# A macaron transformer block (feed-forward, attention, feed-forward) on one core: the list of dense steps by engine clocks in nanoseconds, and six bursts of value products a group for seven

## The chip, the cores and the metric

One core of a Trainium2 chip runs one program. The metric is the device time of an execution in microseconds, the median of the runs shown. The kernel stays in one launch.

## The reference

```python
x = x + 0.5 * ffn(layernorm(x))
x = x + attention(layernorm(x))
x = x + 0.5 * ffn(layernorm(x))            # x: 16 x 1024 x 256, float32

def ffn(x):                                # x_prev: x one position earlier, zeros at the start
    xr = mu_r * x + (1 - mu_r) * x_prev
    xk = mu_k * x + (1 - mu_k) * x_prev
    return sigmoid(xr @ W_r.T) * (square(relu(xk @ W_k.T)) @ W_v.T)

def attention(x):                          # 16 heads of 16, rotary embedding on q and k, causal
    q, k, v = split(x @ W_qkv + b_qkv)
    att = softmax(mask(rope(q) @ rope(k).T / 4))
    return (att @ v) @ W_proj + b_proj
```

## The kernel before

**Attention sets the beat.** Time is laid out in slots, numbered from `FIRST` = -120. A batch has 16 heads in 4 groups of 4; a group has 12 ticks (a block of 128 keys against a block of 512 queries, cut at the diagonal), and each tick 4 slots, one for each head. So a group is 48 slots and a batch 192, 3072 in all. In a slot TensorE makes one score block (`score`, L704, 512, 384, 256 or 128 columns of bf16, with the negated row maximum as extra rows), and one block of the maxima pass of a coming group (`maximum`, L714, the same widths, 13 slots ahead). Scores go to one of NS = 2 PSUM banks (`ps_s`), and ScalarE takes their exponential to `pt_sb` (L830). Maxima go to one of NM = 3 banks (`ps_m`); VectorE takes the row maximum (L943 at the diagonal, L946 elsewhere). GpSimd zeroes what lies above the diagonal (L1075).

**Value products** (`pv`, L735) run in bursts given by `BURSTS`: a burst makes the products of one or two ticks for 4 heads, three slots after the last of its ticks. They are float32, of 32-column weights, and four heads stand side by side in the array. `PT` = 3 tick buffers hold the exponentials.

**Dense steps** fill the rest. All that is not attention's own beat is a step with a name: statistics (`f_st0`, `a_st0`), the reciprocal root on GpSimd (`f_rstd`), normalising on ScalarE to `xt_sb` (`f_x0`, `f_x1`), a transpose (`f_T`, `a_T`, L742), mixing with the position before (`f_dif`, `f_k0` to `f_r1`), the feed-forward matmuls `f_K` (L788), `f_R` (L791) and `f_V` (L794), query and key `r_QK` (L800), value `a_V` (L804), projection `p_P` (L781), the rotary steps (`r_swap`: four DMAs that swap halves, L612; `r_cos`, `r_sin` L997, `r_add` L1001), the split of q and k in three bf16 parts, and DMAs that spread them to rows (`rows`, L627, two each). Each matmul step on a chunk of 256 positions is four units, a unit being 128 x 128 weights on 256 columns, float32, that the profile shows as two matmuls. They use one of ND = 2 PSUM banks, and an ACT or DVE step empties each.

**The planner.** `Plan.describe` (L126) gives every step an engine, a cost in slots, an earliest slot (its release less 16) and the steps it follows, each with a lag in slots. `Plan.place` goes through the slots; every engine earns credit (`RATE`, of TensorE 1.0 a slot) and spends it on the first step by rank whose lags have passed. The outcome is one fixed order for each engine. Each engine's program walks the slots: TensorE does the slot's score, its maximum, the dense units placed there, then a burst if one is due; ScalarE the exponential and then dense steps; VectorE dense steps and then the maximum; GpSimd the diagonal and then dense steps; SP only dense steps, which are DMAs. The planner's times are no waits: at run time each engine waits on semaphores, in order.

## Time and profile before

| | us |
|---|---|
| median of the runs | 3116.66 |
| lowest of the runs | 3114.29 |
| profiled execution, device time | 3112.07 |
| its span, first to last instruction | 3110.3 |

The granted TensorE clock of the profiled execution is 0.991 on the mean. One microsecond is 0.03% of the span. The profile's rows give start, length, engine, line and what is written from what; TensorE's matmuls overlap, since each one is pipelined behind the next, so the distance between starts tells what one costs.

### The profile page before, as it was taken

How to read it: one execution, taken by the hardware profiler on the slowest of the kernel's cores; microseconds unless marked ns; L12 is line 12 of the kernel's file. 1: busy time of each engine (PE TensorE's matmuls, PEld its weight loads, DVE VectorE, ACT ScalarE, POOL GpSimd, SP SyncE). 2: the span in 40 equal slices, each digit the busy share in tenths (PEclk: the TensorE clock that was granted, in tenths of full speed). 3: DMA queues.
4: the chain of work that ended last, by engine and by line, in shares of the span. 5: the costliest groups of instructions: out<-in, count | busy, mean ns of one | idle time of the engine just before them, and what ended most of it. 6: DMA issues, size and time to landing. Idle time of an engine off the chain costs nothing.

```text
span 3110.3 us, 56224 instructions
## 1 busy us (share of the span) xinstructions
PE 2962.3 (95%) x18245; PEld 1665.9 (54%) x18245; DVE 2475.0 (80%) x7302; ACT 2159.2 (69%) x4802; POOL 1566.6 (50%) x2190
## 2 busy tenths in 40 slices
PE   6899999999999999999999999999999999999997
PEld 4444555555555555555555555555555555555444
DVE  3888888888888888888888887888888888887872
ACT  4477777777777777777777777777767777777664
POOL 5455555555455455555555455454555555454323
PEclk9899999999999999999999999999999999999999
DMA  3443343343434352342443333343442532433421
GB/s 99 79 84 65 64 100 66 83 90 72 86 77 88 69 97 67 76 99 60 91 87 68 88 77 84 80 85 76 79 93 59 98 81 67 93 76 71 83 60 39
DMA packets 202585, 245.49 MB, mean 79 GB/s; under 512 B 68405, under 2 KB 104245, under 8 KB 202293
## 3 DMA queue, kind: packets, MB, share of 16 engines
q1 hardware_dynamic: 202293, 241.90, 37.5%
q8 instruction: 146, 2.39, 0.4%
q14 instruction: 146, 1.20, 0.2%
HBM read 53.48 MB, written 51.38 MB: 34 GB/s over the span
## 4 chain that ended last, share of the span: by engine, by line
PE 66%; DVE 12%; ACT 8%; POOL 6%; issue 6%; DMA 1%; SPq 1%; POOLq 0%; DVEq 0%; ACTq 0%
PE ps_y L735 14%; PE ps_s L704 12%; PE ps_m L714 11%; PE ps_d L794 7%; PE ps_d L788 6%; PE ps_d L791 5%; PE ps_d L800 5%; ACT pt_sb L830 4%; DVE ps_m L943 3%; PE ps_d L781 3%; PE ps_d L742 2%; DVE mx_sb L946 2%; PE ps_d L804 2%; POOL pt_sb L1075 2%; DVE dif_sb L974 2%
## 5 line engine op out<-in xcount | busy, mean ns | idle before, releaser
L830 ACT ACTIVATE pt_sb<-ps_s 128x512 f32<-128x512 f32 (+1 forms) x3039 | 1451.6, 495 | 816.9 <-PE ps_s L704 806.7
L943 DVE CUSTOM_DVE_ANT_0 ps_m<-ps_m,mask_sb 128x128 f32<-128x128 f32 (+3 forms) x2048 | 990.3, 498 | 370.7 <-PE ps_m L714 355.9
L704 PE MATMUL ps_s<-qr_sb,kr_sb 99*128 99x512 bf16 (+1 forms) x3039 | 994.5, 329 | 50.4 <-ACT pt_sb L830 39.3
L714 PE MATMUL ps_m<-kr_sb,qr_sb 96*128 96x512 bf16 (+3 forms) x3072 | 1000.1, 329 | 37.9 <-DVE mx_sb L943 27.7
L946 DVE TENSOR_REDUCE mx_sb<-ps_m 128x1 f32<-128x512 f32 x1024 | 697.9, 682 | 105.7 <-PE ps_m L714 97.3
L1075 POOL TENSOR_SCALAR_AFFINE_SELECT pt_sb<-pt_sb 128x512 f32<-128x512 f32 x512 | 331.4, 647 | 833.8 <-ACT pt_sb L830 833.3
L735 PE MATMUL ps_y<-pt_sb,v_sb 128*32 128x512 f32 (+3 forms) x6144 | 589.9, 494 | 3.6 <-POOL pt_sb L1075 2.7
L704 PEld LDWEIGHTS ps_s<-qr_sb,kr_sb 99*128 99x128 bf16 x3039 | 291.8, 96 | 510.0 <-issue 229.7
L714 PEld LDWEIGHTS ps_m<-kr_sb,qr_sb 96*128 96x128 bf16 x3072 | 302.0, 98 | 319.2 <-DVE mx_sb L943 71.1
L800 PE MATMUL ps_d<-axn_sb,wqk_sb 128*128 128x256 f32 x1024 | 305.3, 396 | 3.9 <-ACT axn_sb L872 3.9
L735 PEld LDWEIGHTS ps_y<-pt_sb,v_sb 128*32 128x32 f32 x6144 | 154.6, 109 | 285.9 <-issue 258.3
L788 PE MATMUL ps_d<-ka_sb,wk_sb 128*128 128x256 f32 x1024 | 305.1, 395 | 0.5 <-DVE ka_sb L968 0.5
L791 PE MATMUL ps_d<-wr_sb,dif_sb 128*128 128x256 f32 x1024 | 303.1, 383 | 0.1
L794 PE MATMUL ps_d<-wv_sb,ka_sb 128*128 128x256 f32 x1024 | 301.3, 383 | 0.3 <-ACT dif_sb L865 0.3
L943 DVE DVE_READ_ACCUMULATOR2_ANT mx_sb<- 128x1 f32 x2048 | 286.7, 140 | 0.0
L1116 POOL TENSOR_TENSOR qb_sb<-qb_sb,cos_sb 128x512 f32<-128x512 f32 x124 | 176.2, 1421 | 129.7 <-DMA sw_sb<-qb_sb 129.6
L788 PEld LDWEIGHTS ps_d<-ka_sb,wk_sb 128*128 128x128 f32 x1024 | 189.8, 197 | 52.7 <-issue 2.3
L1103 POOL TENSOR_TENSOR x_sb<-x_sb,dif_sb 128x512 f32<-128x512 f32 x128 | 162.7, 1271 | 100.5 <-DVE dif_sb L980 100.0
L794 PEld LDWEIGHTS ps_d<-wv_sb,ka_sb 128*128 128x128 f32 x1024 | 179.6, 190 | 44.4 <-ACT fxn_sb L854 4.9
L1122 POOL TENSOR_TENSOR part_sb<-qb_sb,part_sb 128x512 bf16<-128x512 f32 x124 | 145.2, 1171 | 114.8 <-ACT part_sb L894 114.3
L800 PEld LDWEIGHTS ps_d<-axn_sb,wqk_sb 128*128 128x128 f32 x1024 | 177.0, 193 | 46.8 <-issue 4.3
L791 PEld LDWEIGHTS ps_d<-wr_sb,dif_sb 128*128 128x128 f32 x1024 | 177.3, 191 | 44.8 <-DVE dif_sb L980 0.5
(96 smaller groups left out, 3465.5 us busy)
## 6 DMA issues: line engine op xcount, KB each, us to landing
kr_sb<-part_sb SPq DMA_DIRECT2D x378, 128.0 KB, 4.4
qr_sb<-part_sb SPq DMA_DIRECT2D x378, 128.0 KB, 4.7
y_way<-yt_sb SPq DMA_DIRECT2D x128, 256.0 KB, 2.7
sw_sb<-qb_sb SPq DMA_DIRECT2D x496, 64.0 KB, 2.0
x_sb<-x SPq DMA_DIRECT2D x64, 256.0 KB, 2.8
yn_sb<-y_way SPq DMA_DIRECT2D x64, 256.0 KB
den_sb<-r_way SPq DMA_DIRECT2D x64, 256.0 KB
out<-x_sb SPq DMA_DIRECT2D x64, 256.0 KB, 2.2
```

What stands on the lines that cost most here:

```text
L704: eng.matmul(score_bank(slot)[:, 0:width], kr_sb[0:KR + NP, n % RS, j, kb * P:(kb + 1) * P], qr_sb[0:KR + NP, n % RS, j, q0:q0 + width], s ...
L714: eng.matmul(ps_m[:, u % NM, 0:width], qr_sb[0:KR, n % RS, j, i * P:(i + 1) * P], kr_sb[0:KR, n % RS, j, piece * QC:piece * QC + width], s ...
L735: pv_j = eng.matmul(ps_y[32 * j:32 * j + 32, QC - width:QC], v_sb[:, b % 2, kb, col:col + 32], pt_sb[:, buffer, j, column:column + width], ...
L788: mm = eng.matmul(ps[:, rows], wk_sb[:, cc, cols], ka_sb[:, i % 2, cc, :], start=(cc == 0), stop=(cc == CC - 1))
L791: mm = eng.matmul(ps[:, rows], dif_sb[:, i % 2, cc, cols], wr_sb[:, cc, :], start=(cc == 0), stop=(cc == CC - 1))
L794: mm = eng.matmul(ps[:, rows], ka_sb[:, i % 2, cc, cols], wv_sb[:, cc, :], start=(cc == 0), stop=(cc == CC - 1))
L800: mm = eng.matmul(ps[:, rows], wqk_sb[:, cc, w0:w0 + P], axn_sb[:, c, cc, :], start=(cc == 0), stop=(cc == CC - 1))
L830: eng.activation(pt_sb[:, buffer, j, column:column + width], score_bank(slot)[:, 0:width], ACT.Exp, scale=SCALE).then_inc(exped, 1)
L943: eng.tensor_tensor_reduce(ps_m[:, u % NM, 0:width], ps_m[:, u % NM, 0:width], mask_sb[:, m0:m0 + width], 1.0, -3e38, ALU.add, ALU.max, be ...
L946: eng.tensor_reduce(best, ps_m[:, u % NM, 0:width], mybir.AxisListType.X, ALU.max).then_inc(max_taken, 1)
L1075: eng.affine_select(out=diag, in_=diag, compare_op=ALU.is_ge, fill=0.0, base=0, pattern=[[0, G], [1, P]], channel_multiplier=-1).then_inc( ...
L1116: eng.tensor_tensor(biased_of(i), biased_of(i), cos, ALU.mult).then_inc(r_cos, 1)
```

## The change

`BURSTS` loses one entry: ticks 0 and 1 of a group go out together.

`Plan.place` is written anew from slot `SWITCH` = 48 on. Up to there the old placing is kept (`place_early`, with the old tests renamed `can_make_at` and `ready_at`). Behind it each engine has a clock in nanoseconds. `TAKES` gives for every step the time that the engine is held and the time after which others see it done; `EXP` and `MAX` give the same for the exponentials and the row maxima, and TensorE's own work goes by columns at 2.36 GHz, with 245 ns a burst. In a slot the new `place` advances TensorE past the score and the maximum (each no sooner than its bank is free by the clocks), places a transpose if its input is seen and a bank is free (`turn`), and then units (`unit`): one if there is one, and more for as long as the next score's or maximum's bank comes free over 150 ns later. The other engines are filled (`fill`) with steps whose predecessors are seen by then, up to a limit and with a slack (`SLACK`): a lower step goes to VectorE only if it ends within 400 ns of the next maximum's being made. `f_R` may now follow the start of `f_K`, `f_V` that of `f_R`, and `y_copy` follows its burst. Some releases move earlier by 4 to 14 slots. The checks that rows and maxima are placed some slots ahead are gone; in their place the clock waits for them. `READER` is renamed `EMPTIER`.

```diff
--- before.py
+++ after.py
@@ -47,7 +47,7 @@
 BSLOTS = NG * GSLOTS
 PV_AT = 3
 PT = 3
-BURSTS = [(0,), (1,), (2, 3), (4, 5), (6, 7), (8, 9), (10, 11)]
+BURSTS = [(0, 1), (2, 3), (4, 5), (6, 7), (8, 9), (10, 11)]
 PLACES = [(k, 0) if TICKS[k][1] != KQ * TICKS[k][0] + KQ - 1 else (k - 1, QC // 2) for k in range(NTK)]
 OWNERS = [k for k in range(NTK) if PLACES[k][0] == k]
@@ -58,6 +58,7 @@
 NH = KQ * G
 UNITS_FIRST = [(i, j, piece) for i in (3, 0, 2, 1, 7, 4, 6, 5) for j in range(G) for piece in range(i // KQ + 1)]
 FIRST = -120
+SWITCH = 48
 HALF_MAX = -53
 REST_MAX = -33
@@ -83,8 +84,24 @@
 class Plan:
 
+    TAKES = {"f_st0": (335, 470), "f_st1": (600, 760), "f_rstd": (1600, 1700), "f_x0": (490, 645), "f_x1": (490, 645), "f_T": (440, 640),
+             "f_xn": (477, 645), "f_dif": (1270, 1330), "f_k0": (397, 530), "f_k1": (397, 530), "f_r0": (397, 530), "f_r1": (397, 530),
+             "f_relu": (477, 665), "f_sq": (500, 675), "f_tanh": (477, 645), "f_u": (600, 735), "f_xadd": (1222, 1330),
+             "a_st0": (335, 470), "a_st1": (600, 760), "a_rstd": (1600, 1700), "a_x0": (490, 645), "a_x1": (490, 645), "a_T": (440, 640),
+             "a_xn": (477, 645), "a_vc": (477, 645), "a_bias": (1222, 1330), "r_b0": (356, 530), "r_b1": (356, 530), "r_swap": (240, 3600),
+             "r_cos": (1350, 1700), "r_sin": (700, 840), "r_add": (603, 740), "r_hi": (519, 680), "r_rest": (1170, 1500), "r_mid": (519, 680),
+             "r_low": (1170, 1500), "store": (60, 2500), "load": (60, 3800), "h_fin": (700, 900), "h_T": (130, 400), "h_copy": (156, 330),
+             "h_rows": (240, 2500), "m_fin": (900, 1000), "m_T": (130, 400), "m_copy": (157, 330), "m_rows": (60, 2500),
+             "y_copy": (477, 645), "y_out": (120, 3500), "y_recip": (159, 300), "y_back": (60, 2700), "y_in": (120, 4500),
+             "y_mul": (1300, 1400), "xp": (604, 740), "b_add": (328, 450)}
+    EXP = {128: (157, 333), 256: (264, 440), 384: (370, 547), 512: (477, 653)}
+    MAX = {128: (192, 410), 256: (330, 535), 384: (465, 670), 512: (600, 800)}
     RATE = {"PE": 1.0, "ACT": 0.5, "DVE": 0.6, "POOL": 0.85, "SP": 1.4}
     AHEAD = {"PE": 1.5, "ACT": 0.5, "DVE": 0.5, "POOL": 0.8, "SP": 1.4}
+    GHZ = 2.36
+    HEARD_PE = 200
+    UNIT = 4 * CH / GHZ
+    TICK = 900
     EARLY = 16
 
...
@@ -120,7 +138,7 @@
             return FIRST + 5 * c + 12 * (c // 2)
         if b == 1:
             return -8 + 16 * c
-        return at - BSLOTS - 44 + 18 * c
+        return at - BSLOTS - 50 + 18 * c
 
...
-            s("PE", "f_R", p, 4, t, ("f_K", p, 0), ("f_r1", p, 3))
+            s("PE", "f_R", p, 4, t, ("f_K+", p, 0), ("f_r1", p, 3))
             s("ACT", "f_tanh", p, 0.47, t, ("f_R", p, 1))
-            s("PE", "f_V", p, 4, t, ("f_R", p, 0), ("f_sq", p, 2))
+            s("PE", "f_V", p, 4, t, ("f_R+", p, 0), ("f_sq", p, 2))
             s("DVE", "f_u", p, 0.61, t, ("f_V", p, 1), ("f_tanh", p, 2))
             s("POOL", "f_xadd", p, 1.2, t, ("f_u", p, 2))
...
-                t = FIRST + 12 + 6 * c + 10 * (c // 2) if b == 0 else (b - 1) * BSLOTS - 10 + 18 * c
+                t = FIRST + 12 + 6 * c + 10 * (c // 2) if b == 0 else (b - 1) * BSLOTS - 16 + 18 * c
                 t_v = t + 100 if b else HALF_MAX - 14 + 3 * c
...
-                        t = (b - 1) * BSLOTS + (104 + 22 * c if pair else -4 + 18 * c)
+                        t = (b - 1) * BSLOTS + (90 + 20 * c if pair else -10 + 18 * c)
                     s("PE", "r_QK", i, 4, t, ("a_xn", b * NCH + c, 2))
...
-                s("ACT", "y_copy", k, 0.48, done + 1, ("y_out", k - NQC, 4))
+                s("ACT", "y_copy", k, 0.48, done + 1, ("y_out", k - NQC, 4), ("pv", k, 0))
                 s("SP", "y_out", k, 1.6, done + 1, ("y_copy", k, 1), ("y_in", m - NQC, 4))
...
             s("SP", "load", i, 1, 4 * (i - 2 * NCH))
 
-    READER = {"f_T": "f_xn", "f_K": "f_relu", "f_R": "f_tanh", "f_V": "f_u", "a_T": "a_xn", "r_QK": "r_b0",
+    EMPTIER = {"f_T": "f_xn", "f_K": "f_relu", "f_R": "f_tanh", "f_V": "f_u", "a_T": "a_xn", "r_QK": "r_b0",
               "a_V": "a_vc", "p_P": "xp", "m_T": "m_copy", "h_T": "h_copy", "b_P": "b_add"}
-
...
+    def T_OF(self, key):
+        return key[0][:2] + "T", key[1]
+
+    def ready(self, now, after):
+        return all(self.done.get((n, i), math.inf) <= now for n, i, lag in after)
+
+    def can_make(self, name, i, slot, now):
+
+        _, cost, _, early, after = self.steps[name, i]
+        _, _, _, early_too, after_too = self.steps[self.EMPTIER[name], i]
+        return early <= slot and early_too <= slot + 4 and self.ready(now, after) and self.ready(
+            now + 3000, [x for x in after_too if x[0] not in (name, "f_tanh")])
+
+    def free_banks(self, now):
+        return [d for d in range(ND) if self.held[d] is None or self.done.get(self.held[d], math.inf) <= now]
+
+    def hold(self, key, d):
+        self.held[d] = "r_b1" if key[0] == "r_QK" else self.EMPTIER[key[0]], key[1]
+        self.bank[key], self.nth[key] = d, self.uses[d]
+        self.uses[d] += 1
+
+    def pick(self, e, slot, now, room=math.inf):
+        best = None
+        for name, line in self.chains.get(e, {}).items():
+            if not line or name[1:] == "_T":
+                continue
+            _, cost, rank, early, after = self.steps[name, line[-1]]
+            if early > slot or not self.ready(now, after) or e != "PE" and rank[0] == 2 and self.TAKES[name][0] > room:
+                continue
+            if name[2:] == "x0" and self.xt is not None and self.done.get(self.T_OF(self.xt), math.inf) > now:
+                continue
+            if e == "PE" and not self.can_make(name, line[-1], slot, now):
+                continue
+            if best is None or (rank, line[-1]) < best[0]:
+                best = (rank, line[-1]), name, line
+        return best and (best[1], best[2].pop())
+
+    def fill(self, e, slot, limit):
+
+        now = self.clock[e]
+        while True:
+            key = self.pick(e, slot, now, limit + self.SLACK[e] - now if now < limit else -1)
+            if key is None and now >= limit:
+                break
+            if key is None:
+                later = self.soonest(e, slot, now)
+                if later > limit:
+                    break
+                now = later
+                continue
+            if key[0][2:] == "x0":
+                self.xt_before[key], self.xt = self.xt, key
+            pace, seen = self.TAKES.get(key[0], (240, 4900))
+            self.at[e][slot].append(key)
+            self.slots[key] = slot
+            self.done[key] = now + seen
+            now += pace
+            self.todo -= 1
+        self.clock[e] = max(self.clock[e], now)
+
+    def soonest(self, e, slot, now):
+
+        times = [math.inf]
+        for name, line in self.chains.get(e, {}).items():
+            if line and self.steps[name, line[-1]][3] <= slot:
+                at = max([self.done.get((n, i), math.inf) for n, i, lag in self.steps[name, line[-1]][4]], default=now)
+                if name[2:] == "x0" and self.xt is not None:
+                    at = max(at, self.done.get(self.T_OF(self.xt), math.inf))
+                if at > now:
+                    times.append(at)
+        return min(times)
+
+    def unit(self, slot, now):
+
+        free = self.free_banks(now)
+        if free and self.current is None:
+            key = self.pick("PE", slot, now)
+            if key:
+                self.hold(key, free[0])
+                self.done[key[0] + "+", key[1]] = now
+                self.current = key, 0
+        if self.current is None:
+            return 0
+        key, u = self.current
+        self.at["PE"][slot].append((*key, u))
+        self.current = (key, u + 1) if u + 1 < self.steps[key][1] else None
+        if self.current is None:
+            self.finish(key, slot, now + self.UNIT + 150)
+        return self.UNIT
+
+    def finish(self, key, slot, now):
+        self.slots[key] = slot
+        self.done[key] = now + self.HEARD_PE
+        self.todo -= 1
+
+    def turn(self, slot, now):
+
+        first = [n for n in ("m_T", "h_T", "f_T", "a_T") if self.chains["PE"][n] and self.can_make(n, self.chains["PE"][n][-1], slot, now)]
+        free = self.free_banks(now)
+        if not free or not first:
+            return now
+        key = first[0], self.chains["PE"][first[0]].pop()
+        self.hold(key, free[0])
+        self.at["PE"][slot].append((*key, 0))
+        pace, seen = self.TAKES[key[0]]
+        self.slots[key] = slot
+        self.done[key] = now + seen
+        self.todo -= 1
+        return now + pace
+
+    def place_early(self):
+
         credit = dict.fromkeys(self.RATE, 0.0)
-        held = [None] * ND
-        uses = [0] * ND
         current, left, xt = None, 0.0, None
-        self.at = {e: {} for e in self.RATE}
-        slot, todo = FIRST, len(self.steps)
-        while todo:
+        held, uses, chains = self.held, self.uses, self.chains
+        for slot in range(FIRST, SWITCH):
             for e in self.RATE:
                 boost = 2.5 if slot < HALF_MAX or slot >= self.nb * BSLOTS else 1.7 if slot < NH else 1.0
...
                     self.slots[key] = slot
                     credit[e] -= self.steps[key][1]
-                    todo -= 1
+        self.current, self.xt = current and (current, int(self.steps[current][1] - left)), xt
...
+    def place(self):
+        self.describe()
+        self.chains = {}
...
+            k, units = score_at.get(slot), units_at.get(slot, ())
+            needs = [(f"rows{NT - 1}" if u >= NH else f"part{NT - 1}", u // NU) for u in units]
+            needs += [] if k is None else [("m_rows" if k >= NH else "h_rows", k // GSLOTS)]
+            while not all(needed in self.done for needed in needs):
+                pe = self.turn(slot - 1, pe)
+                pe += self.unit(slot - 1, pe)
+                pe += 300
+                for e in engines[1:]:
+                    self.fill(e, slot - 1, pe)
+                assert pe < 1e8, needs
+            if k is not None:
+                pe = max(pe, exped.get(k - NS, 0), self.done["m_rows" if k >= NH else "h_rows", k // GSLOTS])
+                qc, kb = TICKS[k // G % NTK]
+                width = QC - max(0, kb - KQ * qc) * P
+                pe += width / self.GHZ
+            scored = pe + self.HEARD_PE
...
+                i, j, piece = UNITS[v] if m else UNITS_FIRST[v]
+                span = min(QC, (i + 1) * P - piece * QC)
+                pe += span / self.GHZ
+                made[u] = span, pe + self.HEARD_PE
+            pe = self.turn(slot, pe)
+            n = 0
+            while True:
+                soon = max(exped.get((k or 0) + 1 - NS, 0), max([taken.get(u + 1 - NM, 0) for u in units], default=0))
+                if n and (HALF_MAX <= slot < n_scores and soon < pe + 150 or pe > now + self.TICK and not HALF_MAX <= slot < n_scores):
+                    break
+                took = self.unit(slot, pe)
+                if not took:
+                    break
+                pe += took
+                n += 1
+            if slot in self.bursts:
+                for n, qc, kb, width, last in self.bursts[slot]:
+                    pe += 4 * width / self.GHZ
+                    if last:
+                        self.done["pv", NQC * n + qc] = pe + 100 + self.HEARD_PE
+                pe += 245
+            self.clock["PE"] = pe
+            now = max(now + self.TICK, pe) if slot < 0 or slot >= n_scores else pe
+            if k is not None:
+                start = max(self.clock["ACT"], scored)
+                pace, seen = self.EXP[width]
+                exped[k] = start + seen
+                self.clock["ACT"] = start + pace
+            self.fill("ACT", slot, now + 400)
+            self.fill("DVE", slot, min([made[u][1] for u in units], default=now))
+            for u in units:
+                span, at = made[u]
+                start = max(self.clock["DVE"], at)
+                pace, seen = self.MAX[span]
+                taken[u] = start + seen
+                self.clock["DVE"] = start + pace
+            if k is not None and k % G == G - 1 and kb >= KQ * qc:
+                self.clock["POOL"] = max(self.clock["POOL"], exped[k]) + 586
+            self.fill("POOL", slot, now)
+            self.fill("SP", slot, now)
             slot += 1
             assert slot < self.nb * BSLOTS + 2000, [k for k in self.steps if k not in self.slots][:20]
         self.end = slot
-        for n in range(self.nb * NG):
-            assert self.slots[f"rows{NT - 1}", n] + 6 <= unit_slot(n * NU + (0 if n else NH)), ("rows", n)
-            assert self.slots["m_rows", n] + 3 <= score_slot(n * GSLOTS + (0 if n else NH)), ("m_rows", n)
-        assert self.slots[f"part{NT - 1}", 0] + 4 <= HALF_MAX, "part"
-        assert self.slots["h_rows", 0] + 3 <= HALF_SCORE, "h_rows"
         for c in range(NCH):
             assert self.slots["a_vc", c] < (score_slot(G) if c < NCH // 2 else NH + G), ("a_vc", c)
         for k in range(self.nb * NG * NQC):
```

## Rows read from the trace of the kernel before

**Rows 1.** The page: busy us (share) x instructions; then PE in 40 slices, in tenths
```profile
PE 2962.3 (95%) x18245; PEld 1665.9 (54%) x18245; DVE 2475.0 (80%) x7302; ACT 2159.2 (69%) x4802; POOL 1566.6 (50%) x2190
PE   6899999999999999999999999999999999999997
```

**Rows 2.** Timeline of TensorE: start us, length us, engine, line, operation, count
```profile
1500.33 0.59 PE L791 MATMUL ps_d<-wr_sb,dif_sb 128*128 128x256 f32 x2
1500.76 0.38 PE L704 MATMUL ps_s<-qr_sb,kr_sb 99*128 99x512 bf16 x1
1500.98 0.38 PE L714 MATMUL ps_m<-kr_sb,qr_sb 96*128 96x512 bf16 x1
...
1503.81 0.60 PE L794 MATMUL ps_d<-wv_sb,ka_sb 128*128 128x256 f32 x2
1504.33 1.92 PE L735 MATMUL ps_y<-pt_sb,v_sb 128*32 128x512 f32 x16
...
1512.42 1.71 PE L735 MATMUL ps_y<-pt_sb,v_sb 128*32 128x512 f32 x16
1514.07 0.23 PE L704 MATMUL ps_s<-qr_sb,kr_sb 99*128 99x128 bf16 x1
...
1514.19 0.65 PE L800 MATMUL ps_d<-axn_sb,wqk_sb 128*128 128x256 f32 x2
1514.68 0.22 PE L704 MATMUL ps_s<-qr_sb,kr_sb 99*128 99x128 bf16 x1
...
1523.97 1.06 PE L735 MATMUL ps_y<-pt_sb,v_sb 128*32 128x512 f32 x8
1524.96 0.28 PE L704 MATMUL ps_s<-qr_sb,kr_sb 99*128 99x256 bf16 x1
...
1528.15 0.85 PE L735 MATMUL ps_y<-pt_sb,v_sb 128*32 128x384 f32 x8
1528.93 0.23 PE L704 MATMUL ps_s<-qr_sb,kr_sb 99*128 99x128 bf16 x1
```

**Rows 3.** Timeline of TensorE: the same transpose of maxima, six batches apart
```profile
1509.80 0.22 PE L768 MATMUL ps_d<-idb_sb,mp_sb 128*96 128x128 bf16 x1
...
2634.70 0.22 PE L768 MATMUL ps_d<-idb_sb,mp_sb 128*96 128x128 bf16 x1
```

**Rows 4.** Timeline of TensorE, a stretch with little dense work; idle before in brackets
```profile
1477.21 0.59 PE L800 MATMUL ps_d<-axn_sb,wqk_sb 128*128 128x256 f32 x2
...
1482.53 0.39 PE L714 MATMUL ps_m<-kr_sb,qr_sb 96*128 96x512 bf16 x1
1483.44 0.63 PE L742 MATMUL ps_d<-id_sb,xt_sb 128*128 128x128 f32 x4 [0.52 <-ACT xt_sb L839]
1483.90 0.38 PE L704 MATMUL ps_s<-qr_sb,kr_sb 99*128 99x512 bf16 x1
...
1484.97 0.39 PE L704 MATMUL ps_s<-qr_sb,kr_sb 99*128 99x512 bf16 x1
...
1486.46 1.13 PE L800 MATMUL ps_d<-axn_sb,wqk_sb 128*128 128x256 f32 x4
```

**Rows 5.** Weight loads by line, 300 to 2900 us: busy, mean ns | idle before
```profile
L714 PEld LDWEIGHTS ps_m<-kr_sb,qr_sb 96*128 96x128 bf16 x2668 | 262.0, 98 | 259.8 <-DVE mx_sb L943 42.9 <-DVE mx_sb L946 8.6 <-issue 0.3
L704 PEld LDWEIGHTS ps_s<-qr_sb,kr_sb 99*128 99x128 bf16 x2668 | 256.3, 96 | 420.3 <-issue 207.9 <-ACT pt_sb L830 152.9
...
L742 PEld LDWEIGHTS ps_d<-id_sb,xt_sb 128*128 128x128 f32 x656 | 70.8, 140 | 51.1 <-issue 31.6 <-ACT qb_sb L881 13.4 <-ACT dif_sb L865 3.9
```

**Rows 6.** One mix: ns min/median/max, then its mean; one swap and its reader
```profile
L968 DVE SCALAR_TENSOR_TENSOR ka_sb<-dif_sb,muk_sb,fxn_sb x256: 392/480/1477, 15.1 to 3096.2; 128x256 f32<-128x256 f32 x128
...
L968 DVE SCALAR_TENSOR_TENSOR ka_sb<-dif_sb,muk_sb,fxn_sb 128x256 f32<-128x256 f32 x256 | 156.9, 616 | 22.9 <-POOL dif_sb L1098 21.8
...
1480.12 2.46 SPq L612 DMA_DIRECT2D sw_sb<-qb_sb  x4
...
1483.98 0.89 DVE L997 TENSOR_TENSOR sw_sb<-sw_sb,sin_sb 128x512 f32<-128x512 f32 x1 [0.47 <-DMA sw_sb<-qb_sb]
```

76 lines of the change are left out of this document (54 added, 22 removed).

## The prediction

> **What bounds the kernel now.** I read the page first: TensorE is busy 95% of the span and 9 tenths or more in every slice but the first two and the last [rows 1]. Nothing else is near that, so time can come only from two places: work that TensorE no longer does, and moments in which its stream stands still. Busy time does not show the second kind, since matmul ends are modelled and overlap. So I went to TensorE's timeline and read starts only.
>
> In a full stretch a score of 512 columns takes 0.22 us from its start to the next start, a dense unit (two passes of 256 float32 columns) 0.43 us, and a score and a maximum of 128 columns together 0.12 us, so 0.06 each [rows 2]; 384 and 256 columns lie between in proportion. A unit behind a 128-column maximum takes 0.49 us instead of 0.43 [rows 2].
>
> Now one batch of 192 slots, priced with these spacings. Scores and maxima: 192 of 512 columns x 0.218 us = 41.9, 64 each of 384, 256 and 128 at 0.165, 0.112 and 0.059 = 21.5, together 63.4 us. Dense: 160 units (8 feed-forward chunks x 12, 8 query-key chunks x 4, 4 value and 4 projection chunks x 4) x 0.433 = 69.3, and 12 transposes x 0.44 = 5.3. Units behind a 128-wide maximum: 28 x 0.05 = 1.5. Value products: the seven bursts of a group take 1.00 + 0.78 + 0.79 + 1.86 + 1.86 + 1.65 + 0.79 = 8.7 us (of one 512 tick 0.99, of one 384 tick 0.78, of 512 and 384 together 1.65 [rows 2]; the rest scaled by columns from these), and each start of a burst stands 0.09 us further behind a dense unit than a score does (0.52 against 0.43 [rows 2]): 4 x (8.7 + 0.6) = 37.4. Sum 177 us.
>
> The measured period is the distance of one repeated instruction, the transpose of a group's maxima, six batches apart: (2634.70 - 1509.80) / 6 = 187.5 us [rows 3]. So TensorE stands still for about 10.5 us in every batch. That is the whole pool for the list of dense steps.
>
> What it looks like: between the dense unit at 1477.21 and the next at 1486.46 there is no dense work but one transpose [rows 4]. The transpose sits in the queue before its input is there: 0.91 us from the maximum ahead of it (0.22 of it work) while ScalarE still writes `xt_sb`. Then two scores of 512 take 1.07 us, because each waits for an exponential to give back one of two banks: 0.53 us a slot where score and maximum need 0.44 [rows 4]. The weight loads say who is waited for: in 2600 us, 153 us before scores for an exponential, 52 us before maxima for VectorE, 51 us before transposes [rows 5]. These overstate the loss (a load waits while the last matmul still streams: 256 us here against 10.5 x 13.9 = 146 by the sum above), but give its proportions: about 6.3, 2.1 and 2.1 us of the 10.5.
>
> **The change, part by part.**
>
> *Six bursts for seven.* Ticks 0 and 1 go out together at the slot where tick 1 went. Two bursts cost 0.99 + 0.78, one costs 1.65, and one entry of 0.09 goes: 0.21 us a group [rows 2], x 64 groups = 13.4 us; rounding in the rows leaves 13 to 16. I take 14. Tick 0's products come four slots later. Its buffer is next needed for tick 4, five slots after the merged burst, and the output bank's copy gets more time, so nothing queues behind it.
>
> *Transposes.* The new list puts one in only when its modelled clock says that both halves of `xt_sb` are visible. Of 2.1 us a batch I take 1.8 as gone; bounds 0 and 2.1.
>
> *Scores and maxima waiting while dense work exists.* The new list keeps adding units in a slot while the next score's or maximum's bank is over 150 ns away by its clocks; the old one hands out about one a slot whatever the engines do. And a chain of small steps (statistics, normalise, transpose, mix) moves by nanoseconds where the old lags were whole slots, near 20 of them from release to the first `f_K`; holes like 1477 to 1486 close sooner. VectorE gets a dense step only when it ends within 0.4 us of the next maximum.
>
> *What can't go.* 160 units and 12 transposes stand against 192 slots, so at least 20 slots have neither, and each slot given two makes another; I take 40. An empty slot cannot pass faster than the two score banks turn, 0.53 against 0.44 us [rows 4], so 40 x 0.1 = 4 us stay. For the list's own errors (below) I leave 2 us more. So 6 of 10.5 us stay and 4.5 go, transposes included. Bounds: nothing gained, and 8.5 gained if empty slots are so scattered that the banks cover them.
>
> *Where it applies.* The first 48 slots keep the old placing; what is left is 3024 / 192 = 15.75 batches, the last of which has less dense work to place: 15.5 x 4.5 = 70 us. The idle of the first two slices and the last is about (0.4 + 0.2 + 0.3) x 78 = 70 us [rows 1]; part is that unchanged placing, part a chain of transfers and small steps at the end that an order hardly shortens. I take 0, with 5 either way.
>
> Releases of the streams move by 6 slots or so; that moves where holes fall, not how much work there is. Numbers of instructions and transfers stay, apart from the order.
>
> **Sum.** Profiled execution 3112.1 (span 3110.3 and 1.8 around it) - 14 - 70 = 3028. The median of the runs, 3116.7, is 4.6 above the profiled one and the fastest 2.2 above, so I say 3030.
>
> **What speaks against the list.** VectorE's mixes of two inputs (`f_k`) have a median of 480 ns but a mean of 616, with single ones of 1477 [rows 6]. The plan books 397 of pace and 530 until seen, the undisturbed value. 32 mixes a batch x 0.14 = 4.5 us, and some 2 us more if `r_sin` and `r_add` stretch alike, are in no clock of the plan. The Trainium skill, GPSIMD Engine Reference, section Key points, has a reason: GpSimd shares its SBUF interfaces with VectorE, and instructions with two SBUF inputs contend; the long mixes agree with it, though no run here isolates it. By that rule the plan's VectorE runs ahead of the real one just when GpSimd is busy, which is the first rival.
>
> The swap of halves: four issues of one `r_swap` take 2.46 us, and VectorE's `r_sin`, which did wait for it, started 1483.98 - 1480.12 = 3.86 us after the first issue [rows 6]. The plan books 3.6 us until seen and 0.24 us of queue time on SP. So a `r_sin` placed as early as allowed waits 0.3 us, and with one `rows` step (two issues at the same 0.6 us each) ahead on SP 1.5 us. Queued behind it on VectorE are the maxima, and TensorE waits for those. Three maximum banks cover about one slot, 0.87 us.
>
> **The rivals.**
>
> 1. *The list gains little*: VectorE's unbooked 6.5 us a batch land on maxima, which TensorE meets as waits. If 3.5 of the 4.5 us are given back, 1 x 15.5 = 15 remain: 3112 - 14 - 15 = 3083, or 3098 with the bursts alone. For it: VectorE is busy 80% [rows 1], and empty slots are where it is tightest. Against: before meets the same stretched mixes, in runs of four, and its losses at maxima are only 2 us.
>
> 2. *Slower*: the early `r_sin` blocks VectorE. There are 120 swaps behind slot 48. Against 84 us of gain it breaks even at 0.7 us of TensorE's time for each, and is 2% slower from (84 + 62) / 120 = 1.2 us. With the full 1.5 us exposed each time: 3028 + 180 = 3208. For it: the wait in the row. Against: the three banks, and a queue on SP in which a batch's 8 swaps x 2.46 and 24 `rows` steps x 1.2 fill only 48 us of 187.
>
> 3. *The list does nearly all it could*: 8.5 of 10.5 us gone: 3112 - 14 - 132 = 2966.
>
> **How the numbers follow.** Likeliest, 2990 to 3054: 0.53. Rival 3, under 2990: 0.10. Rival 1, 3054 to 3115: 0.27. A little slower by rival 2 but within 2%: 0.04; beyond that: 0.06. A measurement of this kernel tells about 2% from no change, here 62 us, so faster than 3054 counts as faster: 0.63; same 0.31; slower 0.06. The range 2985 to 3095 leaves out about 0.08 below and 0.12 above.
>
> **What would show it.** Right: TensorE's weight loads wait for `xt_sb` hardly at all; the loads' idle before scores falls by a third or so; the distance between batches is near 182 us, 1 of it from bursts; 384 bursts; more slots with two units and none with a late transpose. Wrong: VectorE idle before `r_sin` for the swap well over today's, or idle before maxima's weight loads above 52 us in 2600: then rival 2 or 1. If the period stays above 186 us, the step that failed is the one that lets units fill a wait: the waits lie where no unit is ready.

## The result and the profile after

The changed kernel takes 3294.9 us on the median, the kernel before 3115.5 in the same comparison: 1.0588 times, interval 1.0568 to 1.0607. That is 5.9% slower. The prediction was 3030, range 2985 to 3095, with a chance of 0.06 for slower by over 2%. The profiled execution has a span of 3294.5 us (before 3110.3, so 184 us more) at a mean granted TensorE clock of 0.955 (before 0.991). One of the four executions of the kernel before took 6897 us and is left out of the ratio.

The page, its engines and its slices in tenths (compare [rows 1]); `PEclk` is the granted clock:

```profile
PE 3022.9 (92%) x18245; PEld 1708.0 (52%) x18245; DVE 2499.6 (76%) x7302; ACT 2207.8 (67%) x4802; POOL 1592.6 (48%) x2190
...
PE   6899999998999989989999999989999899999897
...
PEclk8899999998999989999999999999999899999998
```

The same 18245 matmuls take a longer span, and dips stand all through the middle, in busy share and clock together. The weight loads by line, 300 to 2900 us, idle before them at the right (compare [rows 5]):

```profile
L926 PEld LDWEIGHTS ps_m<-kr_sb,qr_sb 96*128 96x128 bf16 x2502 | 247.8, 99 | 411.1 <-DVE mx_sb L1155 153.6 <-DVE mx_sb L1158 47.0 <-issue 4.4
L916 PEld LDWEIGHTS ps_s<-qr_sb,kr_sb 99*128 99x128 bf16 x2503 | 242.9, 97 | 346.5 <-issue 181.5 <-ACT pt_sb L1042 107.2
...
L954 PEld LDWEIGHTS ps_d<-id_sb,xt_sb 128*128 128x128 f32 x624 | 79.6, 148 | 24.5 <-issue 6.6 <-ACT mt_sb L1122 0.5 <-DVE dif_sb L1192 0.4
```

Two of the three pools shrank as forecast: transposes 51 to 24.5 us, scores behind exponentials 153 to 107. The third, maxima behind VectorE, went from 52 to 201. What VectorE itself waited for, of the costliest waits (us in total, times, longest):

```profile
DVE ps_m L1155 <- PE ps_m L926: 288.5, 366, 4.6
DVE sw_sb L1209 <- DMA sw_sb<-qb_sb: 197.4, 65, 10.0
```

Before, the second row had a counterpart of 13.7 us, 20 times, longest 1.9:

```profile
DVE sw_sb L997 <- DMA sw_sb<-qb_sb: 13.7, 20, 1.9
```

`r_sin` stood in VectorE's queue before its swapped halves had landed in 65 of 124 cases, and for up to 10 us. Its waits are of two kinds: 13 of them last 7.0 to 10.0 us and make 104 of the 197 us, one in every batch from 615 us on; the other 52 last 3.5 us or less. One of the 13, SP's part of the timeline first (start, length, line, what):

```profile
2810.65 0.65 SPq L884 DMA_DIRECT2D yn_sb<-y_way  x1
2812.66 0.64 SPq L887 DMA_DIRECT2D den_sb<-r_way  x1
2813.35 0.61 SPq L839 DMA_DIRECT2D kr_sb<-part_sb  x1
2814.00 0.61 SPq L839 DMA_DIRECT2D qr_sb<-part_sb  x1
2814.71 2.47 SPq L824 DMA_DIRECT2D sw_sb<-qb_sb  x4
```

VectorE's:

```profile
2816.06 0.14 DVE L1155 DVE_READ_ACCUMULATOR2_ANT mx_sb<- 128x1 f32 x1
2823.60 0.69 DVE L1209 TENSOR_TENSOR sw_sb<-sw_sb,sin_sb 128x512 f32<-128x512 f32 x1 [7.40 <-DMA sw_sb<-qb_sb]
2824.21 0.56 DVE L1155 CUSTOM_DVE_ANT_0 ps_m<-ps_m,mask_sb 128x384 f32<-128x384 f32 x1
```

TensorE's:

```profile
2819.15 0.38 PE L916 MATMUL ps_s<-qr_sb,kr_sb 99*128 99x512 bf16 x1
2824.88 0.61 PE L926 MATMUL ps_m<-kr_sb,qr_sb 96*128 96x512 bf16 x1 [5.35 <-DVE mx_sb L1155]
2825.28 0.63 PE L916 MATMUL ps_s<-qr_sb,kr_sb 99*128 99x512 bf16 x1
2825.71 0.31 PE L926 MATMUL ps_m<-kr_sb,qr_sb 96*128 96x128 bf16 x1
2825.82 0.63 PE L916 MATMUL ps_s<-qr_sb,kr_sb 99*128 99x512 bf16 x1
2826.24 0.63 PE L926 MATMUL ps_m<-kr_sb,qr_sb 96*128 96x512 bf16 x1
```

The swap goes out at 2814.71, behind a `rows` step and a `y_in` (two reads of 256 KB each, of attention's output and of its denominators, which GpSimd's `y_mul` multiplies; SP waited between the two), and its reader starts 8.9 us later; before it was 3.86 [rows 6], the plan books 3.6. VectorE stands for 7.4 us with the maxima queued behind, three maximum banks carry TensorE to 2819.15, and then TensorE stands too. When it comes back, 512 columns take 0.43 us from start to start and not 0.22. The windows of the same moment, of which the columns that matter here are each engine's busy time and, third from the end, the clock:

```profile
core 0: us, PE busy (x) PEld busy (x) DVE busy (x) ACT busy (x) POOL busy (x), PEclk, DMA share, GB/s
2818.00:2824.00 6.00, 1.53 (x8) 0.73 (x6) 0.40 (x1) 1.89 (x4) 1.62 (x2) 1.00 0.72 128
2824.00:2831.00 7.00, 5.55 (x17) 2.31 (x21) 6.38 (x18) 3.51 (x7) 2.81 (x4) 0.52 0.05 11
```

Six microseconds with TensorE busy for 1.53 of them, and then a granted clock of 0.52, that is 1.2 GHz for nearly the whole stretch. The DMA engines were 0.72 busy while VectorE waited and 0.05 afterwards: transfers were under way, and the swap was among the last. So a long wait like this one is paid twice. The second payment is large: a mean clock of 0.955 over 3294.5 us is 148 us of full speed missing, 0.991 over 3110.3 is 28. If TensorE always had work in those stretches, up to 120 of the 184 us are clock.

### The profile page after: what moved, and what is told of

Read it like the earlier page. It is cut to its first block, busy times and chain, and to the rows that moved or that the text cites. A ratio compares the mean times of both kernels' runs of the same rounds, so it can differ in the third digit from the quotient of the medians.

```text
span 3294.5 us, 56238 instructions
## 1 busy us (share of the span) xinstructions
PE 3022.9 (92%) x18245; PEld 1708.0 (52%) x18245; DVE 2499.6 (76%) x7302; ACT 2207.8 (67%) x4802; POOL 1592.6 (48%) x2190
## 4 chain that ended last, share of the span: by engine, by line
PE 64%; DVE 8%; DMA 7%; ACT 6%; issue 6%; SPq 5%; POOL 4%; POOLq 0%; ACTq 0%; DVEq 0%
PE ps_y L947 13%; PE ps_s L916 12%; PE ps_m L926 11%; PE ps_d L1006 6%; DMA sw_sb<-qb_sb 6%; PE ps_d L1000 5%; PE ps_d L1003 5%; PE ps_d L1012 4%; ACT pt_sb L1042 3%; PE ps_d L1016 3%; SPq L824 3%; DVE ps_m L1155 2%; PE ps_d L993 2%; PE ps_d L954 2%; DVE mx_sb L1158 2%
## 5 line engine op out<-in xcount | busy, mean ns | idle before, releaser
L926 PE MATMUL ps_m<-kr_sb,qr_sb 96*128 96x512 bf16 (+3 forms) x3072 | 1023.4, 336 | 170.6 <-DVE mx_sb L1155 136.3
L916 PE MATMUL ps_s<-qr_sb,kr_sb 99*128 99x512 bf16 (+1 forms) x3039 | 1015.1, 337 | 53.6 <-ACT pt_sb L1042 46.9
L1287 POOL TENSOR_SCALAR_AFFINE_SELECT pt_sb<-pt_sb 128x512 f32<-128x512 f32 x512 | 340.0, 664 | 617.6 <-ACT pt_sb L1042 615.1
L947 PE MATMUL ps_y<-pt_sb,v_sb 128*32 128x512 f32 (+3 forms) x6144 | 601.5, 511 | 2.5 <-POOL pt_sb L1287 2.2
L947 PEld LDWEIGHTS ps_y<-pt_sb,v_sb 128*32 128x32 f32 x6144 | 165.4, 112 | 321.1 <-issue 296.4
L1000 PE MATMUL ps_d<-ka_sb,wk_sb 128*128 128x256 f32 x1024 | 321.0, 403 | 2.1 <-ACT fxn_sb L1066 1.4
L1328 POOL TENSOR_TENSOR qb_sb<-qb_sb,cos_sb 128x512 f32<-128x512 f32 x124 | 197.2, 1590 | 167.6 <-DMA sw_sb<-qb_sb 167.4
L1331 POOL TENSOR_TENSOR qb_sb<-qb_sb,part_sb 128x512 f32<-128x512 f32 x124 | 147.6, 1191 | 233.6 <-ACT part_sb L1103 233.6
L1209 DVE TENSOR_TENSOR sw_sb<-sw_sb,sin_sb 128x512 f32<-128x512 f32 x124 | 100.7, 812 | 197.6 <-DMA sw_sb<-qb_sb 197.4
L1000 PEld LDWEIGHTS ps_d<-ka_sb,wk_sb 128*128 128x128 f32 x1024 | 181.2, 197 | 50.5 <-issue 7.3
```

Of the source, the lines that this page charges most:

```text
L916: eng.matmul(score_bank(slot)[:, 0:width], kr_sb[0:KR + NP, n % RS, j, kb * P:(kb + 1) * P], qr_sb[0:KR + NP, n % RS, j, q0:q0 + width], s ...
L926: eng.matmul(ps_m[:, u % NM, 0:width], qr_sb[0:KR, n % RS, j, i * P:(i + 1) * P], kr_sb[0:KR, n % RS, j, piece * QC:piece * QC + width], s ...
L947: pv_j = eng.matmul(ps_y[32 * j:32 * j + 32, QC - width:QC], v_sb[:, b % 2, kb, col:col + 32], pt_sb[:, buffer, j, column:column + width], ...
L1000: mm = eng.matmul(ps[:, rows], wk_sb[:, cc, cols], ka_sb[:, i % 2, cc, :], start=(cc == 0), stop=(cc == CC - 1))
L1287: eng.affine_select(out=diag, in_=diag, compare_op=ALU.is_ge, fill=0.0, base=0, pattern=[[0, G], [1, P]], channel_multiplier=-1).then_inc( ...
L1328: eng.tensor_tensor(biased_of(i), biased_of(i), cos, ALU.mult).then_inc(r_cos, 1)
```

## The experiments

Each run was compared with the kernel before on the same chip; ratios are to it, with a 95% interval. "Idle before r_sin" is VectorE's wait for swapped halves over the whole span.

| run | bursts | list | us | ratio (interval) | idle before r_sin | clock |
|---|---|---|---|---|---|---|
| before | 7 | old | 3114 to 3117 | 1 | 14 | 0.991 |
| e1 | 6 | old | 3165.7 | 1.0155 (1.0139 to 1.0172) | 9 | 0.986 |
| e2 | 7 | new | 3099.0 | 0.9947 (0.9928 to 0.9967) | 75 | 0.986 |
| changed | 6 | new | 3294.9 | 1.0588 (1.0568 to 1.0607) | 197 | 0.955 |
| e3 | 6 | new, swap booked 7000 | 3136.7 | 1.0068 (1.0050 to 1.0087) | 3 | 0.978 |
| e4 | 6 | new, true SP issue times | 3143.5 | 1.0092 (1.0075 to 1.0109) | 82 | 0.982 |
| e5 | 7 | new, swap booked 7000 | 3178.3 | 1.0201 (1.0184 to 1.0218) | 3 | 0.976 |
| e6 | 7 | new, swap booked 5500 | 3163.8 | 1.0155 (1.0140 to 1.0170) | 15 | 0.978 |
| e7 | 8 | old | 3103.5 | 0.9970 (0.9958 to 0.9982) | 17 | 0.990 |
| e8 | 6 | new, r_sin alone 7000 | 3116.2 | 1.0000 (0.9987 to 1.0013) | 13 | 0.985 |
| e9 | 6 | new, swap ahead of rows | 3216.7 | 1.0327 (1.0306 to 1.0348) | 105 | 0.969 |
| e13 | 6 | new, swap ahead of y_in too | 3280.3 | 1.0545 (1.0514 to 1.0575) | 68 | 0.963 |
| e10 | 7 | new, r_sin alone 7000 | 3071.9 | 0.9864 (0.9847 to 0.9881) | 3 | 0.989 |
| e11 | 8 | new, r_sin alone 7000 | 3155.5 | 1.0131 (1.0108 to 1.0155) | 22 | 0.982 |
| e12 | 9 | old | 3117.4 | 1.0002 (0.9992 to 1.0011) | 14 | 0.990 |
| e14 | 7, others | old | 3156.1 | 1.0123 (1.0108 to 1.0138) | 8 | 0.988 |

**Which half of the change.** The bursts alone on the old list:

```diff
-BURSTS = [(0,), (1,), (2, 3), (4, 5), (6, 7), (8, 9), (10, 11)]
+BURSTS = [(0, 1), (2, 3), (4, 5), (6, 7), (8, 9), (10, 11)]
```

> The kernel before with the six bursts alone, the old list of dense steps. The prediction's term stands or falls here: 0.21 us a group, 14 us faster, so about 3101 against 3115 (ratio 0.9955). If the merged burst itself holds something up (a buffer of the exponentials, the output bank's copy), it is 3115 or more.

And the list alone, which is the changed kernel with the other line:

```diff
-BURSTS = [(0, 1), (2, 3), (4, 5), (6, 7), (8, 9), (10, 11)]
+BURSTS = [(0,), (1,), (2, 3), (4, 5), (6, 7), (8, 9), (10, 11)]
```

> The changed kernel with seven bursts again: the new list alone. Theory A (the list does the damage, because VectorE's r_sin stands in its queue before the swapped halves have landed): 3295 + 14, so 3300 to 3315. Theory B (the longer bursts do it): near 3115.

Measured 3165.7 and 3099.0. e1 came out on the far side of its expectation, e2 at neither of its two theories. The bursts, which I had counted as a safe 14 us gained, cost 49; the list by itself is 18 faster. The two do not add: 49 - 18 is 31, and the change lost 179. The list is planned anew for six bursts, and that plan has 197 us of late swaps where the plan for seven has 75 (one wait over 5 us, against 13).

**The late swap.** One number, for both engines that read the swapped halves:

```diff
-"r_swap": (240, 3600)
+"r_swap": (240, 7000)
```

> The changed kernel with one number changed: the list takes the swap of halves as seen 7000 ns after it is issued, not 3600. Theory A: the idle of VectorE before r_sin falls from 197 us to under 40, the stretches of TensorE at half clock mostly go, and the time comes to 3030 to 3080, below the kernel before. Theory C (the loss is in the list at large: VectorE's mixes stretched by GpSimd, paces too short, holes elsewhere): VectorE's wait moves but the time stays above 3200.

> The changed kernel with SP's clock told the truth of issuing: a swap holds SP 2500 ns and is seen after 3900, a rows step holds it 1250, y_out 1150, y_in 1300, y_back and m_rows 600, loads and stores 400. If the late swaps are late because they wait for their turn to be issued, this recovers as much as a booking of 7000 ns does: 3030 to 3090. If they are late because SP waits for other engines at the head of its queue, or because the transfers themselves take 8 us behind others, little comes back: above 3200.

The diff of e4, in `TAKES` (its changed entries alone, put on one line) and in the default that `rows` steps use:

```diff
-"r_swap": (240, 3600), "m_rows": (60, 2500), "y_out": (120, 3500), "y_back": (60, 2700), "y_in": (120, 4500), "store": (60, 2500), "load": (60, 3800)
+"r_swap": (2500, 3900), "m_rows": (600, 2500), "y_out": (1150, 3500), "y_back": (600, 2700), "y_in": (1300, 4500), "store": (400, 2500), "load": (400, 3800)
-            pace, seen = self.TAKES.get(key[0], (240, 4900))
+            pace, seen = self.TAKES.get(key[0], (1250, 4900))
```

e3 gives 3136.7 and an idle of 3 us: 158 of the 179 us come back, so theory A holds for the damage, but not for the gain behind it. e4 gives 3143.5 with 82 us of idle left. It lies between its two outcomes. Eight of its waits before `r_sin` are still over 5 us, 53 us together, so slow landings stay when the issuing is booked rightly; how much of the rest was the time of issuing is not shown, since the list is another one.

Which engine's queue it is, told by a booking for `r_sin` alone:

```diff
-                s("DVE", "r_sin", i, 0.73, t, ("r_swap", i, 6))
+                s("DVE", "r_sin", i, 0.73, t, ("r_swap+", i, 6))
...
             self.done[key] = now + seen
+            if key[0] == "r_swap":
+                self.done["r_swap+", key[1]] = now + 7000
```

> The changed kernel, six bursts, in which only VectorE's r_sin takes the swap as seen after 7000 ns; GpSimd's r_cos keeps 3600. If the damage comes from VectorE's queue, where the maxima stand behind r_sin, this recovers as much as booking 7000 for both did (3137): 3120 to 3160. If GpSimd's wait counts as much, it stays above 3200.

3116.2, all of the 179 us. GpSimd still waits for the swap, 177 us in 99 waits (167 in 75 in the changed kernel), at no visible cost; VectorE may not. 179 us for 184 us of idle taken away is one for one, clock included.

**What the swap waits behind.** Two runs leave every engine's list as it is in the changed kernel and move steps on SP only. In e9 a swap goes ahead of the other steps of its slot; in e13 a `y_in` up to four slots ahead goes behind it as well (the second cut ends before the loop over the steps, which now runs over `at`):

```diff
-                for name, i in plan.at["SP"].get(slot, ()):
+                for name, i in sorted(plan.at["SP"].get(slot, ()), key=lambda step: step[0] != "r_swap"):
```

```diff
+            at = {slot: list(plan.at["SP"].get(slot, ())) for slot in slots}
+            for slot in slots:
+                if slot > 48 and any(step[0] == "r_swap" for step in at[slot]):
+                    for s in range(slot - 4, slot):
+                        moved = [step for step in at[s] if step[0] == "y_in"]
+                        at[s] = [step for step in at[s] if step[0] != "y_in"]
+                        at[slot] += moved
+                    at[slot].sort(key=lambda step: step[0] != "r_swap")
```

> The changed kernel, the lists of all engines the same, but on SP a swap goes ahead of the rows and other steps of its own slot. If the 8 us swaps are late by their turn to be issued (1.25 us for a rows step) and by the rows transfers queued ahead, the idle before r_sin falls from 197 us to under 130 and the time to 3220 to 3260. If what holds them is the y_in of three slots before, nothing moves: 3285 to 3300.

> As the run before, and a y_in that stands up to four slots ahead of a swap goes behind it too. If the two reads of y_in (the yn rows and the broadcast denominators) are what the swap's packets queue behind, the landing of the latest swaps falls from 9 us to 5 or 6, the idle before r_sin under 90 us and the time to 3130 to 3200. If the landing stays, the transfers of the swap are slow for another reason.

e9: 3216.7, idle 105. Taking the other steps of its slot, mostly a `rows` step, out of the swap's way gives back 78 us. e13: the idle falls on to 68, and of the 124 swaps the 97th percentile from first issue to landing falls from 9.3 us (7.1 in e9) to 5.7. So the swap stood behind both: going ahead of its own slot's other steps takes 2.2 us off that percentile, going ahead of the two reads of `y_in` another 1.4. The trace of the changed kernel shows it without a change too: 27 swaps have a `y_in` and a `rows` step as the last issues ahead of them. In 13 the second read of the `y_in` was issued 2.0 to 2.2 us before the swap, and these are the 13 long waits, with landings of 8.5 to 11.1 us; in the other 14 it was issued 4.9 to 6.2 us before, and the swap landed in 4.3 to 7.4 us. The Trainium skill says in DMA: Bandwidth & Descriptors, section Queues, rings and completion order, that all DMAs of one issuing engine share one ring on each of the DMA engines and are consumed in ring order; that agrees. Yet the time is 3280 and not the 3130 to 3200 expected. VectorE's waits of e13 say why:

```profile
DVE qb_sb L1221 <- POOL qb_sb L1336: 113.7, 22, 8.8
DVE sw_sb L1217 <- DMA sw_sb<-qb_sb: 67.7, 61, 2.9
```

`r_add` now waits for GpSimd's `r_cos`, which stands behind the `y_mul` whose `y_in` was put back. One case, in which the two reads went out at 1003.12 and 1003.81:

```profile
1011.62 1.26 POOL L1347 TENSOR_TENSOR yn_sb<-yn_sb,den_sb 128x512 f32<-128x512 f32 x1 [12.97 <-DMA den_sb<-r_way]
1012.84 1.26 POOL L1336 TENSOR_TENSOR qb_sb<-qb_sb,cos_sb 128x512 f32<-128x512 f32 x1
1014.14 0.69 DVE L1221 TENSOR_TENSOR qb_sb<-qb_sb,sw_sb 128x512 f32<-128x512 f32 x1 [8.78 <-POOL qb_sb L1336]
```

The 13 waits of `r_add` over 7 us, one a batch, all have this order before them. The wait moved to the next step in VectorE's queue, 22 times and up to 8.8 us, and cost nearly the same. What matters is not whose data is late but that anything in front of the maxima is.

**A gain from the list.** With seven bursts:

> The new list with seven bursts and the swap booked at 7000 ns. The list with seven bursts took 3099 and had 75 us of VectorE idle before r_sin and 87 us of half clock. If the late swaps cost there what they cost with six bursts (3295 - 3137 = 158 us for 194 us of idle, 0.8 each), this is 3099 - 0.8 x 70 = 3040 to 3060. If the later rows that the longer booking brings (42 us of TensorE before maxima with six bursts) eat it, 3080 to 3110.

> The same with 5500 ns, which is beyond the landing of three swaps in four. Half of the idle before r_sin goes and the rows come less late. If lateness of rows matters, this beats 7000 and comes to 3040 to 3070; if only r_sin's idle matters, it lies between 3099 and the 7000 version.

Both missed, 3178.3 and 3163.8, worse than the list with its late swaps (3099). The idle before `r_sin` is gone (3 and 15 us) and others have come. In e5 TensorE's waits and one of VectorE's show

```profile
PE ps_m L926 <- DVE mx_sb L1155: 41.7, 55, 4.9
PE ps_m L926 <- DVE mx_sb L1158: 40.7, 34, 7.2
PE ps_m L926 <- DMA qr_sb<-part_sb: 27.3, 8, 14.6
DVE qb_sb L1213 <- POOL qb_sb L1328: 31.5, 7, 7.4
```

The third row is absent before and in e2: the rows of q and k, at the end of the chain that the swap heads, come too late for the maxima. The old planner insisted that they be placed 6 slots ahead; the new one has no such test. But 14.6 of its 27.3 us are one wait at 258 us. The costlier waits are the last row's: `r_add` waits for `r_cos` again, in every second batch, 3.7 to 7.4 us each time (in e6 39 us in 10 waits), and the maxima stand behind it: TensorE's 7.2 us of the second row are one of these. The longest:

```profile
1485.43 1.26 POOL L1339 TENSOR_TENSOR yn_sb<-yn_sb,den_sb 128x512 f32<-128x512 f32 x1 [10.54 <-DMA den_sb<-r_way]
1486.65 1.26 POOL L1328 TENSOR_TENSOR qb_sb<-qb_sb,cos_sb 128x512 f32<-128x512 f32 x1
1487.95 1.73 DVE L1213 TENSOR_TENSOR qb_sb<-qb_sb,sw_sb 128x512 f32<-128x512 f32 x1 [7.35 <-POOL qb_sb L1328]
```

This is e13's order: `r_cos`, booked later together with `r_sin`, has come to stand behind a `y_mul`. It stands so before 6 of e5's 7 waits and before all 7 of e6's over 4 us. The plan books 4.5 us for a `y_in`; where e5's `y_mul` had to wait for one, it started 7.8 us after the first read's issue (median of 46; 5.8 in the kernel before, 17 cases). That these waits make up the loss against e2 is argued from their size, not tested by a run with `y_in` booked later. The later booking for `r_sin` alone keeps `r_cos` early, and there:

> The new list with seven bursts, and only r_sin booked at 7000 ns, as it brought six bursts from 3295 to 3116. The seven-burst list had 75 us of idle before r_sin; if most of that goes and no other order goes bad, 3050 to 3080. If a new list means another set of accidents each time, it lies anywhere from 3060 to 3170, as the two versions with the swap booked longer for both engines did (3178, 3164).

> The same with eight bursts (ticks 4 and 5 apart). On the old list eight bursts were 10 us faster than seven and six were 50 slower. If short bursts help by letting the banks refill, this is 5 to 15 us below the run before; if only the accidents of the list count, the difference has either sign and is larger.

e10 takes 3071.9: 1.4% faster than the kernel before, the fastest of all and within the 3050 to 3080 expected, and `r_add` waits for `r_cos` once (2.3 us). It is also 44 us faster than e8, the same booking with six bursts, so the merge costs on the new list about what it costs on the old. Its weight loads in the same window as [rows 5]:

```profile
L928 PEld LDWEIGHTS ps_m<-kr_sb,qr_sb 96*128 96x128 bf16 x2730 | 267.9, 98 | 271.5 <-DVE mx_sb L1157 35.7 <-DVE mx_sb L1160 5.7 <-DMA qr_sb<-part_sb 1.9
L918 PEld LDWEIGHTS ps_s<-qr_sb,kr_sb 99*128 99x128 bf16 x2731 | 262.0, 96 | 384.7 <-issue 200.0 <-ACT pt_sb L1044 129.7
...
L956 PEld LDWEIGHTS ps_d<-id_sb,xt_sb 128*128 128x128 f32 x660 | 78.8, 140 | 27.4 <-ACT mt_sb L1124 11.8 <-ACT fxn_sb L1068 0.2
```

All three pools are smaller than before (41, 130, 27 against 52, 153, 51). e11, the same with ticks 4 and 5 apart, is 84 us slower than e10, though that split helps the old list. Its VectorE waits 63 us for GpSimd's `f_dif` (33 in e10), up to 5.6 us at a time. So a small edit of the input turns out another list with other late arrivals, and 3072 to 3178 is the spread of such accidents with seven bursts.

**Why the merged burst costs.** TensorE's timeline of e1, around the place where tick 0 had its burst:

```profile
1503.77 0.27 PE L714 MATMUL ps_m<-kr_sb,qr_sb 96*128 96x256 bf16 x1
...
1504.52 0.28 PE L704 MATMUL ps_s<-qr_sb,kr_sb 99*128 99x256 bf16 x1 [0.25 <-ACT pt_sb L830]
1505.13 0.28 PE L714 MATMUL ps_m<-kr_sb,qr_sb 96*128 96x256 bf16 x1 [0.33 <-DVE mx_sb L943]
...
1506.46 0.39 PE L714 MATMUL ps_m<-kr_sb,qr_sb 96*128 96x512 bf16 x1 [0.38 <-DVE mx_sb L943]
1506.78 2.89 PE L735 MATMUL ps_y<-pt_sb,v_sb 128*32 128x512 f32 x16
1509.60 0.29 PE L704 MATMUL ps_s<-qr_sb,kr_sb 99*128 99x128 bf16 x1
1509.68 0.42 PE L714 MATMUL ps_m<-kr_sb,qr_sb 96*128 96x256 bf16 x1
1509.90 0.31 PE L704 MATMUL ps_s<-qr_sb,kr_sb 99*128 99x128 bf16 x1
```

and of the kernel before at the same slots:

```profile
1477.81 0.27 PE L714 MATMUL ps_m<-kr_sb,qr_sb 96*128 96x256 bf16 x1
1478.01 1.07 PE L735 MATMUL ps_y<-pt_sb,v_sb 128*32 128x512 f32 x8
1479.01 0.28 PE L704 MATMUL ps_s<-qr_sb,kr_sb 99*128 99x256 bf16 x1
...
1480.50 0.39 PE L714 MATMUL ps_m<-kr_sb,qr_sb 96*128 96x512 bf16 x1 [0.17 <-DVE mx_sb L943]
1480.82 0.85 PE L735 MATMUL ps_y<-pt_sb,v_sb 128*32 128x384 f32 x8
```

From the same maximum to the next burst it is 3.01 us before (1480.82 - 1477.81), with 1.00 us of tick 0's burst inside, and 3.01 us in e1 (1506.78 - 1503.77), with none. Tick 0's burst cost nothing there: scores and maxima of 256 columns need 0.22 us a slot of TensorE and more of ScalarE and VectorE, so TensorE spent the time on value products or spent it waiting. Moved four slots on, the same work is paid in full. And here the burst takes 2.82 us where 1.65 is right [rows 2], since the clock fell: the 256-column maximum at 1509.68 takes 0.22 us to the next start, not 0.11. This is the rule and not one case. Over 60 groups of both traces (all but the first and last two), it is 7.03 us on the mean before and 6.87 in e1 from the first score of tick 1 to the burst that holds tick 1; group for group the difference is 0.00 on the median, so taking tick 0's burst out of that stretch saves 0.16 and not 0.99. The burst itself then takes 1.64 us instead of 0.78 in 54 groups, and 2.5 to 3.1 in the six where the clock had fallen: 0.97 more on the mean. That makes 0.81 us a group, and no other stretch of the group changes by more than 0.02; the times say 49 / 64 = 0.77. Up to 16 of the 49 us are clock (0.986 against 0.991).

Is it length or place? Each run's `BURSTS`, with the run's name put behind it:

```diff
+BURSTS = [(0,), (1,), (2, 3), (4,), (5,), (6, 7), (8, 9), (10, 11)]              # e7
+BURSTS = [(0,), (1,), (2, 3), (4,), (5,), (6,), (7,), (8, 9), (10, 11)]         # e12
+BURSTS = [(0, 1), (2, 3), (4,), (5,), (6, 7), (8, 9), (10, 11)]                  # e14
```

> The kernel before with ticks 4 and 5 in bursts of their own, eight bursts for seven. Theory D (a burst is time in which ScalarE has two banks and VectorE three to eat and then idles, so a longer one costs more than its saved edge): 64 x 0.23 = 15 us of edges are paid and as much or more comes back, 3085 to 3120. Theory E (only the edges count; the merge of ticks 0 and 1 hurt for a reason of its own place in the group): 3132.

> The old list with nine bursts: ticks 4, 5, 6 and 7 each in one of their own. Theory D (the length of a burst costs, because the two score banks and three maximum banks run dry during it): a second split gives what the first gave, another 10 us, so 3090 to 3098. Theory E' (eight bursts helped by their place only): the second split costs its edges, 3110 to 3120.

> The old list with ticks 0 and 1 merged and ticks 4 and 5 split: seven bursts, as before, at other places. If each burst's length and place acts by itself, the effects add: 3166 - 10 = 3150 to 3160. If only the number of bursts counted, 3115. If the merge hurts because the bursts around it are long too, well under 3150.

Splitting ticks 4 and 5 gains 10 us although it adds 64 edges, which is in theory D's range and not at theory E's 3132; splitting 6 and 7 as well loses 10 (by the ratios, 1.0002 against 0.9970) to 14 (by the medians), or 0.16 to 0.22 us a group, about the bare price of an edge. A second split that gives nothing back speaks against theory D: length by itself does not cost, place does. e14 is 3156.1: 3165.7 - 10, so the effects add up on a fixed old list, and seven bursts at other places are not seven bursts. Why the split at 4 helps and at 6 doesn't I have not shown.

## Why the prediction was wrong

**What bounds the kernel** held: TensorE's stream and its stand-stills, some 10.5 us a batch. So did the edge of a burst, forecast at 0.21 us a group: in e1 the stretch that loses tick 0's burst is 1.09 us shorter and the merged burst 0.86 us longer, which leaves 0.23.

**"Six bursts for seven", 14 us gained**: failed, measured 49 lost. The step that failed is the sentence that nothing queues behind the later burst. It looked at who waits for the burst and did not ask what the burst had covered. The rows had it: in [rows 4]'s stretch TensorE waits on banks between the bursts, so an item of TensorE's work standing there is free, and moving it away saves nothing and costs its length where it lands: 0.86 us a group at full clock.

**Transposes, 1.8 us a batch**: about right in direction; the idle before them halved (51 to 24.5 us in the window).

**Scores and maxima, 4.5 us a batch in all, 70 us**: the list alone gained 18, and 45 with `r_sin` booked later. The mechanism exists (e10's three pools), but I sized it at the clocks' word. The forecast of 6 us left a batch included 2 for errors of the list. In e10 most batches take 183.4 to 184.8 us where the kernel before takes 187.5 (the repeated transpose of the maxima again), so some 3.6 of the forecast 4.5 us a batch are there once nothing stands long in front of the maxima.

**Rival 2 was the case, at a chance of 0.06**, and the sum put it at nothing beyond those 2 us a batch: this is the largest step that failed, 179 us by e8. Its place was right: `r_sin` in front of the maxima on VectorE. Its price was wrong twice. I capped one wait at 1.5 us, from one swap that landed in 3.86 us, and added a `rows` step's issue; I didn't ask what happens when transfers of `rows` and a `y_in` go out just ahead. The latest swap landed after 6.8 us before and 11.1 us in the changed kernel, and the old list's lag of 6 slots hid what lateness there was. Single waits were up to 10 us. And I priced a wait at its length. The clock adds to it: up to 120 us of 184. The point of 2% slower, 1.2 us for each of 120 swaps, was reached: 197 us of idle are 1.6 each. More than half of them come as 13 waits of 7 to 10 us, beyond what three banks cover; e2, with 75 us of idle and one wait over 5 us, was still faster than the kernel before.

**The three together.** 14 forecast for the merge and 49 lost, 70 forecast for the list and 45 found, and 179 for the late swap: 63 + 25 + 179 = 267 us, where 3295 measured and 3030 forecast are 265 apart. Each term comes from runs with a list of their own, so the closeness is in part luck.

**Rival 1** (stretched mixes) remains untested by itself; no run booked the mixes longer.

**The signs named** did their work: VectorE's idle before `r_sin` and the idle before maxima's loads (201 against the 52 named) point to rival 2 at once. The third sign misled: a batch takes some 200 us, above the 186 named, yet the step tied to it, that units fill waits, is not the one that failed, as e10 shows.

**Open**: how the loss splits between waits and clock beyond the upper bound; and whether a list with `y_in` booked at its real landing too would be free of the long waits. The runs show that booking the swap later is not enough.
